# A 512-stage recurrence with a mixture-of-experts feed-forward beside it: TensorE work dealt in smaller pieces, padding matmuls removed, a shorter setup

## The reference

```python
def _derivative(q, p, drive, coupling, bias):
    i_couple = jnp.tanh(q) @ coupling.T
    dq = q - q ** 3 / 3.0 - p + drive + i_couple + bias
    dp = EPSILON * (q + ALPHA - BETA * p)
    return (dq, dp)
```

```python
sh = _silu_and_mul(x @ Ws_gate_up, I_SH) @ Ws_down
shared_out = sh * jax.nn.sigmoid(x @ W_sgate.T)
gu = jnp.einsum('th,ehi->eti', x, We_gate_up)
h = _silu_and_mul(gu, I_MOE)
eo = jnp.einsum('eti,eih->eth', h, We_down)
sparse_out = jnp.einsum('eth,te->th', eo, combine)
```

## Time and profile before

| | |
|---|---|
| median of 3 runs | 664.38 us (664.13 to 665.31) |
| the profiled execution | 664.56 us, of which the span of the trace is 662.6 us |
| busy share of the span | PE 96%, DVE 93%, ACT 54%, POOL 29% |
| mean granted TensorE clock | 0.979 of full |

### The profile page before, as it was taken

One profiled execution on the slowest core, in us unless ns is written; L12 is line 12 of the kernel. 1 busy time (PEld: TensorE's weight loads), 2 busy tenths in 40 slices (PEclk: granted clock), 3 DMA queues, 4 the chain that ended last, 5 costly groups with the idle time before them and its releaser, 6 DMA issues.

```text
span 662.6 us, 33930 instructions
## 1 busy us (share of the span) xinstructions
PE 639.3 (96%) x12847; PEld 609.1 (92%) x12847; DVE 619.2 (93%) x4542; ACT 359.5 (54%) x1860; POOL 194.5 (29%) x436
## 2 busy tenths in 40 slices
PE   3789999999999999999999999999999999999998
PEld 2578899999999999999999999999999999999997
DVE  6899999999999999999999999999999999999951
ACT  2756555646555554655555465555556555555643
POOL 0001123242322324232332423233342323334244
PEclk9975799999999999999999999999999999999999
DMA  8800000000000000000000000000000000000000
GB/s 301 270 2 2 3 3 3 12 3 12 2 12 3 3 12 3 11 3 12 2 3 12 3 11 4 11 3 3 12 3 12 3 12 2 4 12 2 12 2 17
DMA packets 8628, 13.65 MB, mean 21 GB/s; under 512 B 1521, under 2 KB 7985, under 8 KB 8209
## 3 DMA queue, kind: packets, MB, share of 16 engines
q1 hardware_dynamic: 8464, 11.50, 5.3%
HBM read 9.40 MB, written 2.10 MB: 17 GB/s over the span
## 4 chain that ended last, share of the span: by engine, by line
PE 90%; DVE 7%; ACT 2%; issue 1%; DMA 0%; POOL 0%; DVEq 0%; SPq 0%
PE up_ps L561 28%; PE down_ps L576 21%; PE coup_ps L503 15%; PE coup_ps L509 13%; PE coup_ps L492 5%; PE coup_ps L496 3%; PE route_ps L541 2%; DVE w L701 2%; ACT hidden L368 1%; PE route_ps L522 1%; DVE q L777 1%; DVE th_lo L749 0%; DVE force L760 0%; DVE square_ps L746 0%; DVE square_ps L742 0%
## 5 line engine op out<-in xcount | busy, mean ns | idle before, releaser
L561 PE MATMUL up_ps<-q_hi,w 128*128 128x128 f16 x2176 | 238.3, 220 | 0.2 <-POOL q_lo L855 0.2
L892 POOL TENSOR_TENSOR hidden<-hidden,comb_s 128x128 f32<-128x128 f32 x272 | 123.3, 456 | 296.8 <-ACT th_hi L390 289.5
L390 ACT ACTIVATE th_hi<-q 128x32 f16<-128x32 f32 x384 | 88.0, 229 | 223.1 <-DVE q L777 222.2
L561 PE MATMUL up_ps<-q_lo,w 128*128 128x128 f16 x1088 | 201.3, 220 | 0.0
L503 PE MATMUL coup_ps<-th_hi,c 128*128 128x16 f16 x4096 | 181.1, 170 | 1.5 <-ACT th_hi L390 0.8
L576 PE MATMUL down_ps<-hidden,wd 128*128 128x128 f32 x1088 | 180.8, 290 | 0.0
L561 PEld LDWEIGHTS up_ps<-q_hi,w 128*128 128x128 f16 x2176 | 177.4, 98 | 0.7 <-POOL q_lo L855 0.4
L503 PEld LDWEIGHTS coup_ps<-th_hi,c 128*128 128x128 f16 x4096 | 139.1, 96 | 6.8 <-ACT th_hi L390 2.2
L576 PEld LDWEIGHTS down_ps<-hidden,wd 128*128 128x128 f32 x1088 | 141.8, 191 | 0.0
L509 PE MATMUL coup_ps<-th_lo,c 128*128 128x16 f16 x2048 | 131.2, 172 | 1.6 <-DVE th_lo L749 1.5
L431 ACT ACTIVATE act_s<-up_ps,unscale 128x128 f32<-128x128 f32 x272 | 99.2, 365 | 14.5 <-PE up_ps L561 10.5
(11 more groups left out here) (95 smaller groups left out, 1079.3 us busy)
## 6 DMA issues: line engine op xcount, KB each, us to landing
wf<-in_w_up SPq DMA_DIRECT2D x1, 4224.0 KB, 13.5
wd<-in_w_down SPq DMA_DIRECT2D x1, 2048.0 KB, 23.3
out<-out_s SPq DMA_DIRECT2D x16, 128.0 KB, 2.2
xs<-in_x SPq DMA_DIRECT2D x1, 1920.0 KB, 19.7
sel<-in_spread SPq DMA_DIRECT2D x1, 408.0 KB, 19.2
cf<-in_coupling SPq DMA_DIRECT2D x1, 256.0 KB, 2.6
xs<-in_x SPq DMA_DIRECT2D x1, 128.0 KB, 2.3
ident<-in_identity SPq DMA_DIRECT2D x1, 64.0 KB, 2.4
```

The lines of the kernel that those rows point to most:

```text
L390: nc.scalar.activation(th_hi[:], q[:], ACT.Tanh).then_inc(hi_ready, 1)
L561: last = nc.tensor.matmul(up_ps[(f * TILES + j) % UPS][:, h * TOK:(h + 1) * TOK], w16[:, part, k, h, j * P:(j + 1) * P], q[:, k, :], start ...
L892: nc.gpsimd.tensor_tensor(hidden[:, j, :], hidden[:, j, :], comb_s[:, j, :], ALU.mult).then_inc(weighed, 1)
```

## The change

- **Up tiles.** `UP_AT` is replaced by `UPS_IN`, the number of single up matmuls in each stage (mostly 8, where stages before had 12, 6 or none). `SILU_AT` follows from it, `HIDE_AT` and `SPREAD_AT` move by a stage in places.
- **Down tiles.** `DOWN_AT[j]` is now a pair, a stage for each output half m. The last tile's halves are in stages 46 and 47, where before the whole tile was in 46. `FINISH_AT` stays at 48 and 49.
- **Unread matmuls.** `WARM` and its matmuls are gone.
- **Weights.** The scale is made in three DVE instructions, so `HI_AT` is one stage earlier, and two of the 34 `w_lo` pieces move from block 1 into block 0.
- **Setup.** The condition is loaded once (ACT's queue) instead of three times (SP's), `ident_u` moves to ACT, `c_un` to POOL, `p_now` into the time in which DVE waits for PE, and ACT takes the first tanh before it biases the drive.

```diff
-UP_AT = [(2, 2), (3, 3), (4, 4), (6, 6), (8, 8), (9, 10), (11, 11), (12, 12), (13, 13), (15, 15), (16, 16), (17, 18),
-         (20, 20), (22, 22), (23, 24), (26, 26), (27, 28)]
+UPS_IN = [0, 0, 12, 8, 4, 8, 8, 8, 8, 8, 8, 8, 8, 10, 4, 7, 12, 8, 3, 8, 4, 8, 8, 8, 4, 8, 8, 8, 8, 0, 0, 0]
-DOWN_AT = [18, 19, 21, 23, 24, 25, 27, 28, 29, 30, 31, 33, 37, 39, 41, 42, 46]
+DOWN_AT = [(18, 18), (19, 20), (21, 22), (23, 24), (25, 26), (27, 28), (29, 29), (30, 30), (31, 31), (31, 33),
+           (33, 35), (36, 36), (37, 38), (39, 40), (41, 42), (43, 44), (46, 47)]
 FINISH_AT = [STAGES + 16, STAGES + 17]
-WARM = [min(6, max(0, 11 - units(st))) for st in range(STAGES)]
-HI_AT = MOST_AT + 5
+HI_AT = MOST_AT + 4
-         + [STAGES + s for s in (0, 1, 2, 3, 4, 6, 7, 9, 10, 16, 17, 23, 24)])
+         + [STAGES + s for s in (0, 1, 2, 3, 4, 6, 9, 13, 16, 17, 23)])
...
-            sync.dma_start(q_raw[:], cond).then_inc(in_core, 16)
-            sync.dma_start(q_trace[:, :, STEPS - 1, :], cond).then_inc(in_core, 16)
-            sync.dma_start(p_first[:], cond).then_inc(in_core, 16)
+            act.dma_start(q_raw[:], cond).then_inc(in_core, 16)
+            act.dma_start(bias_s[:], bias).then_inc(in_core, 16)
...
-                if n > STAGES:
-                    for _ in range(WARM[st - 1]):
-                        nc.tensor.matmul(coup_ps[:, 2 * P:3 * P], c16[:, 0, 0, 0:P], c16[:, 0, 0, 0:P],
-                                         start=False, stop=True, skip_group_check=True)
...
+                for i in range(UP_FROM[st], UP_FROM[st] + UPS_IN[st]) if st < STAGES else ():
+                    j, h, k, product = i // UP_MMS, i // (3 * KC) % 2, i // 3 % KC, i % 3
...
+                    for m in range(KC):
+                        if DOWN_AT[j][m] == st:
+                            pe.wait_ge(weighed, f * TILES + j + 1)
...
-            step(nc.vector.tensor_scalar(ident_u[:], ident[:], scale[:, 0:1], None, ALU.mult))
-            for k in (0, 2, 3):
-                last = nc.vector.tensor_scalar(c_un[:, k:k + 1], unscale[:, 0:1], C[k], None, ALU.mult)
-            step(last)
```

More of the change, by code:

```diff
@@ L396, in tanh @@
                         act.wait_ge(q_clipped, t)
-                    nc.scalar.activation(square_first, q0_of(st // 4), ACT.Square, scale=SQUARE).then_inc(squared, 1)
+                    nc.scalar.activation(square_first, q0_of(st // 4) if t else q_raw[:], ACT.Square, scale=SQUARE).then_inc(squared, 1)
             def ffn(f, st):
@@ L568, in ffn @@
-                for j in range(TILES):
-                    if DOWN_AT[j] == st:
-                        pe.wait_ge(weighed, f * TILES + j + 1)
-                        if j == 0 and not first_block:
-                            pe.wait_ge(out_ready, KC * f)
-                        for m in range(KC):
+                for i in range(UP_FROM[st], UP_FROM[st] + UPS_IN[st]) if st < STAGES else ():
+                    j, h, k, product = i // UP_MMS, i // (3 * KC) % 2, i // 3 % KC, i % 3
+                    n = i % UP_MMS
+                    if i == 0:
+                        pe.wait_ge(q_split, (KC + 1) * (f + 1))
+                    if n == 0:
+                        if first_block:
+                            pe.wait_ge(w_hi_ready, j + 1)
+                            pe.wait_ge(w_lo_ready, 2 * (j + 1))
+                        if not (first_block and j < UPS):
+                            pe.wait_ge(hidden_ready, f * TILES + j - UPS + 1)
+                    part, q = ((0, q_hi), (0, q_lo), (1, q_hi))[product]
+                    last = nc.tensor.matmul(up_ps[(f * TILES + j) % UPS][:, h * TOK:(h + 1) * TOK],
+                                            w16[:, part, k, h, j * P:(j + 1) * P], q[:, k, :],
+                                            start=n % (3 * KC) == 0, stop=n % (3 * KC) == 3 * KC - 1)
+                    if n == UP_MMS - 1:
+                        last.then_inc(up_ready, 1)
@@ L576, in ffn @@
+                for j in range(TILES):
+                    for m in range(KC):
+                        if DOWN_AT[j][m] == st:
+                            pe.wait_ge(weighed, f * TILES + j + 1)
+                            if j == m == 0 and not first_block:
+                                pe.wait_ge(out_ready, KC * f)
                             last = nc.tensor.matmul(down_ps[:, m * TOK:(m + 1) * TOK],
@@ L708, in scan_stage @@
                 t = b * STEPS + i
-                q = q_in[k][:] if k else q0_of(i)
+                q0 = q0_of(i) if t else q_raw[:]
+                q = q_in[k][:] if k else q0
                 def add(out, q, factor, to):
@@ L732, in scan_stage @@
                 elif k == 1:
-                    add(y3[:], p_now[:], P_IN_Y3, q0_of(i))
+                    add(y3[:], p_now[:], P_IN_Y3, q0)
                 elif k == 2:
@@ L847, in _ @@
         def _(pool):
-            pool.wait_ge(setup_v, SETUP_V)
+            pool.wait_ge(setup_v, 5)
+            for k in (0, 2, 3):
+                nc.gpsimd.tensor_scalar(c_un[:, k:k + 1], unscale[:, 0:1], C[k], None, ALU.mult
+                                        ).then_inc(c_un_ready, 1)
             def ffn(f, st):
```

131 lines of the change are left out of this document (57 added, 74 removed).

## The result

The changed kernel takes **662.88 us** (median of 16 runs, 662.78 to 663.36), the kernel before 664.39 in the same session (16 runs; one of them took 1221.1 us and is left out of the comparison). The ratio is 0.9975, interval 0.9968 to 0.9983: 1.5 us **faster**, a small change, but its interval leaves out 1. The forecast was 665.1 us, with slower as the likeliest direction. The time is inside the range of 662.5 to 672.6, the direction is not the one that had the highest chance.

A forecast was written before the change was run, and what follows sets the result against it. Each stage was taken as a latency chain of 1.18 us with 0.79 us of PE room for feed-forward work. 664.56 - 2.4 + 3.8 + 0.7 - 1.4 + 0 = 665.26, against the median 665.1 us; range 662.5 to 672.6.

The forecast's parts named there:

- Blocks 0 and 1 ... Taken together **0**, bounds -0.6 and +0.4: First two blocks: moved `w_lo` pieces cost block 0 +0.6 to +0.8, block 1 gains -0.4 to -1.2; together 0 us.
- -0.4 to -1.2: Block 1: two whole `w_lo` pieces fewer and some stages of twelve up matmuls at the low clock spared, in us.
- Dealing, -2.4: Blocks 2 to 15: even up and down work gives back 0.035 in five stages a block, -2.4 us.
- The last half, +3.8: Stage 16, 14 blocks: `finish_chunk` waits for the last down half, `out_s` 0.27 later each time, +3.8 us.
- worth 0 in the chain: Unread matmuls between the drive matmuls and the wait for `th_hi`: they used spare PE time, so removal gains 0.
- Tail, +0.7: Behind stage 511: 1.5 more down tiles fall into the PE-bound tail at 0.48 each, +0.7 us.
- Setup, -1.4: Before the first q: fewer small instructions, three moved off DVE's chain, an earlier first reduction; -1.4 us, bounds -1.2 and -1.6.
- the 0.2 for the identity matrix: Setup: the first reduction no longer waits for the identity matrix; 0 to 0.4 us gained, 0.2 taken.
- so the stage that waits for it should not take this back: Setup: the up weights' transfer is issued earlier, so the stage waiting for it should not undo the setup's gain.
- The wait at finish is not there: Rival, stage 16: the last half is ready when DVE asks, so 3.8 goes away, 661.3 us; chance 0.15.
- The clock falls: Rival, around stages 31 to 1: without unread matmuls PE's clock drops, +1.5 us a fall, 672.6 to 686; chance 0.24.
- Blocks 1 and 2 stay at the low clock longer: Rival: PE regains the high clock later; some 15 stages at 1.3 instead of 1.18, +1.8, 666.9 us; chance 0.13.

The follow-up runs named there:

- weights_as_before: The changed kernel with the `w_hi` and `w_lo` stages of before (HI_AT one later, LO_AT of before): 662.72 us, ratio 0.9978 to the kernel before.
- deal_only: The kernel before with only the new up, down, hide and spread tables; unread matmuls, weight pieces and setup kept: 668.82 us, ratio 1.007.
- deal_no_unread: The kernel before with the new tables and without the unread matmuls; setup and weight pieces as before: 665.09 us, ratio 1.0014.
- the square above: Medians, us: old tables with unread matmuls kept 664.07, gone 673.44; new tables kept 668.82, gone 665.09; all with the old setup.
- tail_grouped: `last_tile_in_14` with the two halves of a down tile run together behind stage 511: 659.14 us, ratio 0.9923 to the kernel before.
- setup_only: The kernel before with only the new setup; tables, unread matmuls and weight stages as before: 662.82 us, ratio 0.998.
- last_tile_in_14: The changed kernel with both halves of the last down tile in stage 14, that stage's four up matmuls moved to stage 15: 659.42 us, ratio 0.993.
- half_less_at_31: `last_tile_in_14` with one down half less at stage 31 and four up matmuls moved from stage 3 to 4: 672.16 us, ratio 1.0117.
- no_unread_only: The kernel before without the unread matmuls, nothing else changed: 673.44 us, ratio 1.0137.
- whole_tiles: The changed kernel with whole down tiles at the stages of before, 12 or 4 up matmuls in many stages, some hide stages moved: 675.36 us, ratio 1.0172.
- half_less_unread_back: `half_less_at_31` with three unread matmuls given back in each of stages 30, 0, 1 and 2: 661.79 us, ratio 0.9965 to the kernel before.
- up_weights_alone: `last_tile_in_14` with the transfers behind the up weights held back until these have landed: 659.76 us, ratio 0.9933 to the kernel before.

## Why the prediction missed the direction

The step that failed is "Blocks 0 and 1 ... Taken together **0**, bounds -0.6 and +0.4". They gave -1.5 (-2.28 in block 1, +0.82 in block 0; without the late transfer -1.9). Less the 0.26 that belongs to the setup's term, that is -1.2 to -1.65 in place of 0; with this alone put right the forecast would have been 663.9 to 663.4 us, below the kernel before instead of above it. Of block 0's +0.82, 0.45 is the late transfer and -0.26 belongs to the setup, so the edit itself cost +0.6 to 0.7, within the +0.6 to +0.8 forecast. Block 1's "-0.4 to -1.2" was where it went wrong: `weights_as_before` puts 0.74 on the pieces, `deal_only` 1.1 on the dealing (0.85 of it in stages 12 and 13, which take 1.25 each there although the granted clock is low from 72.4 to 75.8 and both lie in that stretch: eight up matmuls nearly fit at 1.2 GHz where twelve, at 1.68, don't) and `deal_no_unread` another 0.4 on the unread matmuls, part of it because its clock does not fall again in these two stages. The sentence named the low-clock stages of twelve and gave them at most 0.4 beside the pieces, although the prediction had worked out 1.3 for a stage of eight at the low clock itself: two stages at 1.68 - 1.3 make 0.8. (The three parts, 0.74, 1.1 and 0.4, make 2.2 of the 2.28.)

The other terms, by their own steps:

- **Dealing, -2.4.** Right, in mechanism and size. The stages behind the five overfull ones (10, 11, 19, 25, 29) went from 1.21 to 1.18, 0.032 each and 2.25 in all. Blocks 2 to 15 as a whole moved by +0.33, of which the finish is +2.9 and isolated long stages (below) are -0.2, which leaves -2.4.
- **The last half, +3.8.** Mechanism and place right, `out_s` 0.04 later than forecast. The size was too large by 0.9, the second largest error of the sum: it was 0.22 a block and not 0.27, and 13 blocks and not 14, +2.9. In block 9 `out_s` was 0.31 later, `th_lo` 0.26 (it started 0.21 behind `out_s` instead of the 0.26 of the earlier trace rows), and the next q 0.22. Why each step takes a little back was not tried.
- **Unread matmuls, "worth 0 in the chain".** Right only for the place from which they were removed. By the square above they were worth 9.4 us in the old tables, through the clock, and would have cost 3.7 to 3.9 in the new ones.
- **Tail, +0.7.** It was +1.24. The step counted 1.5 tiles at the price of a long run and left out what separation costs. PE's timeline of after's tail:

```profile
634.74 0.44 PE L566 MATMUL down_ps<-hidden,wd 128*128 128x128 f32 x2
635.02 0.22 PE L553 MATMUL up_ps<-q_hi,w 128*128 128x128 f16 x1
...
635.46 0.66 PE L566 MATMUL down_ps<-hidden,wd 128*128 128x128 f32 x4
635.96 0.28 PE L553 MATMUL up_ps<-q_hi,w 128*128 128x128 f16 x2
```

A lone half among up matmuls takes 0.28, two together 0.50, and in a long run it is 0.226 each. `tail_grouped` wins 0.26 of this back; the other 0.3 above the forecast was not taken apart.

- **Setup, -1.4.** Right in sum: 1.4 by `setup_only`. It came otherwise than said: the 0.2 for the identity matrix was not there (the reduction starts at 3.62, by 0.07 later), and 0.26 came in stage 15 of block 0.
- "**so the stage that waits for it should not take this back**": in the profiled execution it did take back 0.45. The transfer was issued 2.3 us earlier but took 2.0 us longer (15.5 against 13.5).

Put together for the profiled executions: 664.56 - 2.4 + 2.9 + 1.24 - 1.4 - 1.2 - 0.2 (isolated long stages) - 0.15 (outside the span) = 663.35, measured 663.36. Here -1.2 is the -1.5 of blocks 0 and 1 without the 0.26 counted in the setup. The close agreement proves little, since the remainder of blocks 2 to 15 was put down to the dealing.

**The rivals.** "The wait at finish is not there" fell: the wait is there, in 13 of 14 blocks. "The clock falls" did not happen, but it was the right thing to fear: starting from `last_tile_in_14`, one more down half moved (`half_less_at_31`) brings it about, and so does removing the unread matmuls from the old tables alone. Its forecast price of 1.5 a fall was nearly twice what was measured (0.8 in `no_unread_only`, 0.9 in `half_less_at_31`), and in the fall shown for `no_unread_only` three stages are long, by 0.29, 0.47 and 0.19. "Blocks 1 and 2 stay at the low clock longer" had the wrong sign: the granted clock is low from 40.8 to 68.1 us in one piece now against 42.5 to 63.0 and 69.8 to 76.7 before, the same length in all, but block 1 became 2.28 shorter.

## What to carry to other kernels

Before a piece of work is split to fill a stage evenly, look at who waits for its *last* piece: here one half moved one stage later cost 3.0 us, more than the 2.3 to 2.4 that the even filling brought. Padding matmuls and the load around them are one edit, not two: in this kernel the new tables alone cost 4.8 us and the removal alone 9.4, both together 0.9. Look at the clock's row of each step, since PE's busy share did not show what was coming. A phase at the low clock has prices of its own, so work its stages out one by one instead of taking two short blocks together as zero.

## What the runs showed of the hardware

- TensorE's granted clock fell from 2.4 to 1.2 GHz between 100 and 637 us although its records showed it busy for 99.9% of that stretch, in the profiled executions of `no_unread_only`, `whole_tiles` and `half_less_at_31` (11, 10 and 12 falls). It never fell there in those of the other kernels, two of which differ from `half_less_at_31` little: `last_tile_in_14` by one down half and four up matmuls moved, `half_less_unread_back` by twelve unread matmuls a block.
- A stage with twelve up matmuls took 1.68 us at the low clock (stages 12 and 13 of block 1, before) and one with eight 1.25 (`deal_only`), against 1.18 for both at the high clock.
- The clock's row reads 9 in the first slices, yet it was not high from the start: in the kernel before the unread matmuls of block 0 start 0.106 us apart until about 35.7 us, 0.055 from there to 42.5, and 0.107 behind it, where the granted clock is low. In these traces the row says nothing before its first recorded change.
- The kernels whose clock held have seven isolated long stages in blocks 2 to 15, 0.06 to 0.32 longer than the same stage of other blocks, 0.9 to 1.3 us in all. Stage 5 of block 9 is one in after (369.77 to 371.17) and in `setup_only` (+0.22). Kernels that differ little have them at the same places: after, `last_tile_in_14`, `weights_as_before`, `up_weights_alone`, `tail_grouped` and `half_less_unread_back` share all seven; before has others. In after DVE stands idle for 0.21 us in that stage, and nothing that the profile records ends the wait. What causes them was not found.
- The transfer of the up weights took 13.1 to 13.5 us from issue to landing where it was issued at 4.4 us and 14.3 to 15.5 where it was issued at 2.1; holding the transfers behind it back did not shorten it (15.4).
